# Selective scans in four directions: y's columns gathered by ScalarE before TensorE starts a fold, and z's matmul placed ahead of the sums of its half item

## What is computed

```python
xs = jnp.stack([xr, xc, jnp.flip(xr, -1), jnp.flip(xc, -1)], axis=1)     # rows, columns, and back
x_dbl = jnp.einsum('bkdl,kcd->bkcl', xs, x_proj_w)                       # dts, Bs, Cs
dt = jax.nn.softplus(dts + dt_bias[None, :, :, None])
def step(h, inp):
    ut, dtt, bt, ct = inp
    dA = jnp.exp(dtt[..., None] * A)
    h = dA * h + (dtt * ut)[..., None] * bt[:, :, None, :]
    y = jnp.einsum('bkdn,bkn->bkd', h, ct)                               # 16 states n
    return (h, y)
ys = ys + Ds.reshape(1, K, D_INNER, 1) * xs
y = ys[:, 0] + col2row(ys[:, 1]) + jnp.flip(ys[:, 2], -1) + col2row(jnp.flip(ys[:, 3], -1))
```

## Time and profile before

| | us |
|---|---|
| median of 3 executions | 28529.37 |
| lowest, highest | 28515.41, 28530.03 |
| profiled execution | 28593.1 |
| its span, first to last instruction | 28591.4 |

### The profile page before, as it was taken

One profiled execution on the slowest core, in us unless ns is written; L12 is line 12 of the kernel. 1 busy time (PEld: TensorE's weight loads), 2 busy tenths in 40 slices (PEclk: granted clock), 3 DMA queues, 4 the chain that ended last, 5 costly groups with the idle time before them and its releaser, 6 DMA issues. The chain is left out here.

```text
span 28591.4 us, 600844 instructions
## 1 busy us (share of the span) xinstructions
PE 27059.4 (95%) x242880; PEld 20043.6 (70%) x242880; DVE 25875.7 (91%) x24430; ACT 18929.7 (66%) x37728; POOL 23415.0 (82%) x10688
## 2 busy tenths in 40 slices
PE   8999998998999999899899999989989999998998
PEld 6776775774677677577467767757746776775774
DVE  8998997997899899899789989979978998997997
ACT  6775775774677577577467757757746775775774
POOL 7996995994799699599479969959947996995994
PEclk9999999999999999999999999999999999999999
DMA  3332332331333233233133323323313332332331
GB/s 106 102 101 80 105 105 80 106 110 44 101 104 100 82 103 105 80 109 108 45 100 105 99 82 102 105 80 108 108 45 100 105 99 82 102 105 80 108 108 45
DMA packets 3552030, 2679.50 MB, mean 94 GB/s; under 512 B 3255348, under 2 KB 3258636, under 8 KB 3294584
## 3 DMA queue, kind: packets, MB, share of 16 engines
q1 hardware_dynamic: 489912, 2628.56, 25.9%
q10 hardware_dynamic: 3059328, 12.24, 6.2%
HBM read 2541.99 MB, written 111.15 MB: 93 GB/s over the span
## 5 line engine op out<-in xcount | busy, mean ns | idle before, releaser
L971 POOL TENSOR_TENSOR regB<-regB,regA 128x1024 f32<-128x1024 f32 x9216 | 21517.9, 2376 | 618.8 <-ACT carry L838 607.4
L932 DVE TENSOR_TENSOR_SCAN regB<-regB,carry,ps 128x512 f32<-128x512 f32 x16128 | 19137.1, 1257 | 243.6 <-PE ps L730 215.8
L849 ACT ACTIVATE regB<-regB,a_neg 128x512 f32<-128x512 f32 x18432 | 12184.1, 710 | 0.6 <-issue 0.2
L730 PEld LDWEIGHTS ps<-regA,regB 64*128 64x128 f32 x147456 | 8999.2, 188 | 3536.0 <-issue 2923.7
L730 PE MATMUL ps<-regA,regB 64*128 64x128 f32 x147456 | 10741.4, 285 | 104.7 <-DVE regB L932 59.1
L744 PE MATMUL ps<-ident,regB 128*128 128x128 f32 x73728 | 10082.7, 280 | 229.1 <-POOL regB L971 163.3
L744 PEld LDWEIGHTS ps<-ident,regB 128*128 128x128 f32 x73728 | 7905.5, 141 | 1407.4 <-POOL regB L971 397.9
L838 ACT ACTIVATE carry<-regB 128x2 f32<-128x2 f32 x9216 | 1888.8, 205 | 6151.6 <-DVE regB L932 5617.7
L961 POOL TENSOR_TENSOR regB<-regB,u 128x512 f32<-128x512 f32 x1152 | 1635.0, 1419 | 1972.2 <-DVE regB L915 1972.2
L932 DVE TENSOR_TENSOR_SCAN regB<-regB,ps 128x512 f32<-128x512 f32 x2304 | 2617.4, 1200 | 229.2 <-PE ps L730 193.8
L705 PE MATMUL ps<-regB,dt_w 13*128 13x512 f32 (+1 forms) x2304 | 1274.5, 633 | 171.8 <-SPq L667 171.8
(11 more groups left out here) (103 smaller groups left out, 13630.7 us busy)
## 6 DMA issues: line engine op xcount, KB each, us to landing
regA<-c SPq DMA_DIRECT2D x1536, 1024.0 KB, 4.7
regA<-eye SPq DMA_DIRECT2D x384, 2048.0 KB, 7.7
regA<-x_in SPq DMA_DIRECT2D x16, 1536.0 KB, 13.5
x_keep<-regA SPq DMA_DIRECT2D x8, 3072.0 KB, 17.6
regA<-x_keep SPq DMA_DIRECT2D x16, 1536.0 KB, 13.9
regB<-xd SPq DMA_DIRECT2D x128, 192.0 KB
regB<-w_in_in SPq DMA_DIRECT2D x28, 576.0 KB, 11.5
xd<-regB SPq DMA_DIRECT2D x64, 192.0 KB
```

The lines of the kernel that those rows point to most:

```text
L730: mm = nc.tensor.matmul(b.rearrange("p (t s) -> p s t", s=2), dtuT[at, up, q, :], diag[at, cp, q, g], start=True, stop=True)
L849: nc.scalar.activation(decays[:, g % 2, s], dt[:, up, :], ACT.Exp, scale=a_neg[:, c[0], d, 2 * g + s:2 * g + s + 1]).then_inc(a_made, 1)
L932: nc.vector.tensor_tensor_scan(ring[:, g % RING, s, way], decays[:, g % 2, s, way], b[:, s, way], 0.0 if begun else carry[:, d, at:at + 1] ...
L971: nc.gpsimd.tensor_tensor(ring[:, g % RING], ring[:, g % RING], c_all[:, g], ALU.mult).then_inc(g_made, 1)
```

## The change

In the columnwise directions ScalarE copies the chunk of y for the coming fold into a contiguous buffer `y_col`, the first 512 columns of `xd_odd`. It does so at half item g = 1 (ACT_COL) of the unit after, behind the decays, with a semaphore of its own (`col_made`). `start_y` waits for it and reads `y_col` as moving operand in place of the columnwise view; the identity as stationary operand and the place in PSUM stay. The gather waits for `y_kept` (y's chunk as the direction before left it) and for `y_mm` (the fold before the last has been finished, so the buffer may be overwritten). Behind the last unit it stands ahead of `keep_yT`. Rowwise directions have no gather. In all directions `project_dt` at g = 1 moves from behind `sums` to ahead of it.

```diff
--- before.py
+++ after.py
@@ -39,7 +39,7 @@
 QS = T // (ROWS * RT)
 EYE = QS * NS * RT
 PE_LAG, PE_Z, PE_SKIP, PE_Y, PE_TR = 3, 1, 4, 5, 6
-ACT_B, ACT_IN, ACT_LOG, ACT_YT, ACT_Y, ACT_TR = 4, 2, 3, 3, 6, 7
+ACT_B, ACT_COL, ACT_IN, ACT_LOG, ACT_YT, ACT_Y, ACT_TR = 4, 1, 2, 3, 3, 6, 7
 DVE_DT = 3
 POOL_DTU = 3
 PW = W + 2
@@ -607,7 +607,7 @@
             M = R + 2 * NS
             (c_q0, c_q1, c_q2, c_q3, dts_loaded, spread_b,
              z_mm, sp_abs, sp_exp, sp_ln, sp_half, dt_made, dtu_made, tr_mm, dtT_made, diag_loaded,
-             a_made, b_made, scanned, carried, g_made, yT_mm, yT_kept, y_mm, y_kept, dw_loaded) = sems[:26]
+             a_made, b_made, scanned, carried, g_made, yT_mm, yT_kept, y_mm, y_kept, dw_loaded, col_made) = sems[:27]
             c_loaded = (c_q0, c_q1, c_q2, c_q3)
             Y_BANK, Z_BANK, T_BANK = 4, 6, 7
             LAST = chunk_of(K - 1, NCH - 1, NCH // 2 - 1)
@@ -631,6 +631,12 @@
             def following(this, after, d):
 
                 return (this, d + 1) if d + 1 < NDB else after and (after, 0)
+
+            y_col = xd_odd[:, 0:T]
+
+            def col_unit(c, d):
+
+                return (c[0] // 2 * NCH + c[1]) * NDB + d
 
             def unit(c, d):
                 return c[3] * NDB + d
@@ -754,6 +760,10 @@
                         pe.wait_ge(yT_kept, U + 1)
                         if k == 0:
                             w, src = skip_w[:, d, :], u
+                        elif k % 2:
+                            pe.wait_ge(col_made, col_unit(c, d) + 1)
+                            nc.tensor.matmul(ps[:, Y_BANK + up, :], ident[:], y_col, start=True, stop=False)
+                            return
                         else:
 
                             w, src = ident[:], y_acc
@@ -779,10 +789,10 @@
                             nxt = following(this, after, d)
                             for g in range(PAIRS):
                                 inputs(this, d, g, (par + d) % 2, par)
+                                if nxt and g == PE_Z:
+                                    project_dt(*nxt)
                                 if (old := behind(this, before, d, g, PE_LAG)):
                                     sums(*old, par_of(old[0], par, this, old[1]))
-                                if nxt and g == PE_Z:
-                                    project_dt(*nxt)
                                 if g == PE_SKIP and (old := behind(this, before, d, 0, PAIRS)):
                                     start_y(old[0], old[1], par_of(old[0], par, this, old[1]))
                                 if g == PE_Y and (old := behind(this, before, d, 0, PAIRS)):
@@ -857,6 +867,15 @@
                         wait(act, y_mm, U)
                         nc.scalar.activation(yT, ps[:, Y_BANK + up, :], ACT.Copy).then_inc(yT_kept, 1)
 
+                    def gather_y(c, d):
+
+                        k, n, _, S = c
+                        if k % 2 == 0:
+                            return
+                        act.wait_ge(y_kept, unit(c, d) - NDB + 1)
+                        act.wait_ge(y_mm, unit(c, d))
+                        nc.scalar.activation(as_chunk(y_col, k), in_order(y_acc, k, d, n), ACT.Copy).then_inc(col_made, 1)
+
                     def keep_y(c, d, up):
 
                         k, n, _, S = c
@@ -884,6 +903,8 @@
                                 if (old := behind(this, before, d, g, 2)):
                                     keep_last(*old)
                                 make_decays(this, d, g, (par + d) % 2)
+                                if g == ACT_COL and (old := behind(this, before, d, 0, PAIRS)):
+                                    gather_y(old[0], old[1])
                                 if nxt and g == ACT_IN:
                                     softplus_in(*nxt)
                                 if nxt and g == ACT_LOG:
@@ -899,6 +920,7 @@
                     chunks(act, step)
                     for g in (PAIRS - 2, PAIRS - 1):
                         keep_last(LAST, NDB - 1, g)
+                    gather_y(LAST, NDB - 1)
                     keep_yT(LAST, NDB - 1, NDB % 2)
                     keep_y(LAST, NDB - 1, NDB % 2)
```

## The result

| | us | ratio to before |
|---|---|---|
| before, median of 6 (28515.4 to 28535.9) | 28529.7 | |
| changed, median of 6 (28288.0 to 28310.0) | 28301.2 | 0.9921 [0.9908, 0.9934] |
| forecast | 28300 | |

The account below looks back on a forecast made before the run. TensorE's own work was taken to bound the columnwise units, with GpSimd's 20.08 us next. Terms of 190 + 29 + 10 = 229 us off the median 28529.4 gave 28300 us, range 28180 to 28440.

Parts of the forecast that it names:

- What bounds: Columnwise units: TensorE's own gapless work of 20.56 us holds the scans; without it GpSimd's 20.08 comes next.
- the rule on weight loads: TensorE judged by weight loads, 78% busy columnwise: VectorE would bound both directions; rival of 0 to 40 us gain, chance 0.09.
- three engines within 0.01 us: Columnwise unit with TensorE off the path: claimed the three engines nearly equal, naming VectorE 20.07 and GpSimd 20.08 us.
- Part 1: Start of y in columnwise units: contiguous read takes a unit from 20.51 to 20.18 us, 190 us over 576 units.
- 10 at the ends of scans: End of each of 12 scans: the last start of y is on the path, 0.85 us shorter, 10 us in all.
- Part 3: z's matmul ahead of the sums fills their wait for GpSimd: 0.05 us in 576 rowwise units, 29 us.
- GpSimd's wait of 0.10 us a unit: Columnwise units: GpSimd's remaining wait for ScalarE, taken as 0.3 us a chunk; ends 0 and the present 0.39 a unit.
- Part 2: Gather on ScalarE in columnwise units: 576 activations of 1.06 us each, hidden, so no cost to the time.
- The cover: Behind the gather: 0.9 us of ScalarE's idle time plus 0.7 us of GpSimd's lag hide its time.
- the rival for the slower side: Gather on ScalarE's path delays GpSimd; decides from a price of about 2.0 us, 28760 us at 2.4; chance 0.05.
- the rival with all engines at their floors: Both kinds of unit fall to their floors, some 360 us, 28170 us; rowwise includes half of 0.27 us as 30; chance 0.15.
- The third of 0.14 us a unit: Rowwise units: share of the sums' wait for GpSimd that the new order wins, taken as 0.05 us a unit.

Follow-up runs that it names:

- e1: The kernel before with only z's matmul moved ahead of the sums: 28503.3 us, ratio 0.9993 to before.
- e2: The changed kernel with the old order of z's matmul, so gather and contiguous read alone: 28366.4 us, ratio 0.9943 to before.
- e5: The kernel before, unedited, profiled a second time: the execution took 28524.8 us, against 28593 in the first profile.
- e4: The changed kernel with the two DMA issues of B moved from ScalarE's queue to SyncE's: 28117.3 us, ratio 0.9858 to before.
- e11: The changed kernel with GpSimd's dt*u reading u rowwise in the columnwise directions (output not the reference's): 28242.5 us.
- e3: The changed kernel without the gather, TensorE reading a contiguous stretch of y instead (output not the reference's): 28305.9 us.
- e6: The changed kernel with a second, unused copy of y's columns in each gather: 28399.2 us.
- e9: The kernel before with the two DMA issues of B moved from ScalarE's queue to SyncE's: 28349.4 us, ratio 0.9939 to before.

## Why the prediction was right, point by point

**What bounds.** Shown. TensorE bounded the columnwise directions by its own work: e1 leaves them at 20.50 with TensorE at 367.00, e2 takes them to 20.22. By the rule on weight loads (the Trainium skill, Perfetto Trace Analysis, section Identifying the Most-Contended Engine) VectorE would have been the limit; the loads were 78% busy and the engine was full all the same. The page gives them as a measure of the headroom to TensorE's peak, which is another question than which engine the others wait for. Here the share of matmuls and the pitches were the better sign, and the measurement decides. What the prediction calls three engines within 0.01 us are two, VectorE at 20.07 and GpSimd at 20.08; by its own sum TensorE is at 19.71.

**Part 1, 190 us and 10 at the ends of scans.** With the gather alone (e2 against e5) the columnwise directions give 169 us in the traces. With the order beside it they give 210, and the 41 between belong to part 3. So the part was sized 20 us too large. The step in it that was chosen, GpSimd's wait of 0.10 us a unit, was right for the gather alone: all the gaps ahead of its products in the columnwise chunks 1 to 7 of e2 are 0.37 us a chunk for k = 1 and 0.26 for k = 3, 0.10 a unit. In the changed kernel they are 0.16 and 0.10 us a chunk, 0.04 a unit. What was too low was the limit itself, 20.08 where GpSimd's work averages 20.11 (e4). In the changed kernel 20.11 and 0.04 give the measured 20.16, and the two misses nearly cancel against the forecast 20.08 + 0.10 = 20.18. What I had argued only, that GpSimd no longer catches up and so hides the late L838, can be read: for k = 1 its product of item 0 starts 1.5, 1.6 and 1.4 us behind the scan's end in the three blocks, where it was 0.6, 1.4 and 0.9 in e5. e11 shows that its own work was the limit, with VectorE close below.

The 10 us at the ends don't show. Where TensorE's granted clock is 1.00 the last start of y does fall from 1.79 to 0.96 us. But GpSimd's last product now ends 3.4 us behind the last scan instead of 2.7, since GpSimd runs further behind. From the last scan's end to the last write of y are 7.9 us in the changed kernel and 8.0 before. At some scans the granted clock had fallen below 1.00 there, and the same stretch then takes up to 9.4 us before and 10.1 after.

**Part 2, nothing.** Forecast 1.06 us, measured 1.09. The cover held (e3). In the rival for the slower side the mechanism was right and the numbers weren't: I had it decide at a price of 2.0 us, and at 2.1 (e6) the kernel was still 0.4% faster than before. The point lies between two copies and three. In the rival with all engines at their floors a sum was wrong too: half of 0.27 us over 576 units is 78 us, not 30, so that it should have stood near 28110 us.

**Part 3, 29 us.** The rowwise directions give 22 from profile to profile and some 30 at like length of the DMA issues (e1), all of it in the second block of a chunk. The third of 0.14 us a unit was a guess that came out well: I spread the waits over several half items and didn't see that they stood behind the DMA issue. The step that failed is its columnwise half: I let the order give nothing there because TensorE's work stays the same. That holds for the kernel before, and not once part 1 has taken TensorE off the path: there it gives some 40 us in the columnwise units, e2 against the change. So the split was wrong though the sum was right, and that the two errors made up for each other was luck: in the times of e1, e2 and the change it is 160 for the gather, 23 for the order and some 40 for both together, where I had 200, 29 and nothing.

**The profiled execution against the median.** I subtracted the same 229 us from both. From the first profile the distance would have been 293 us of span (28591.4 to 28298.4). The 65 us between belonged to that execution of the kernel before, most of them in the rowwise directions with their longer DMA issues (e5). They were no part of the change, and taking the difference from the median was what kept them out.

## To carry to other kernels

When three engines have nearly the same work in a unit, the gain from unloading one is the distance to the next one's end-to-end time, not the work removed: 490 us of TensorE work went, and for that alone 160 us came out of the time. Put an added operation where its engine waits anyway, and ask what the engine behind it has in hand. Look at what else an engine's queue carries: the DMA issues in ScalarE's program cost this kernel some 180 us, nearly as much as the change gave, and in e4 and e9 SyncE issued them without a wait that the stretches show. Two parts of a change can also draw on the same wait, so measure each alone and both together before you share out the gain.

## What the runs showed of the hardware

A float32 read of 512 elements on 128 partitions costs TensorE 594 ns a pass contiguous, 613 with every second element and 1070 with every fourth; ScalarE needs 658 and 1126 for the latter two. I hadn't expected step 4 to be dearer than step 64 (1026 and 1084 in the same direction). The second DMA issue of a chunk on ScalarE's queue took 3.96 us in a rowwise chunk of the kernel before and 2.66 in a columnwise one of the changed kernel:

```profile
1011.03 2.66 ACTq L227 DMA_DIRECT2D eye<-b  x1
```

Over the whole changed kernel it took 3.4 us on average in both rowwise directions, and 3.1 and 2.8 in the columnwise ones. Why it differs by direction stays open. On SyncE's queue it took longer, 4.4 to 4.9 us on average by direction, and neither stretch of e4 lists a wait for what SyncE loads behind it. One of them:

```profile
1480.03 3.46 SPq L227 DMA_DIRECT2D eye<-b  x1
```
